# First stage of an AdaLN transformer block: q, k, v from two fp32r parts in three products, the norm on ScalarE, statistics two units ahead

## The chip, the core and the metric

The kernel runs on one core of a Trainium2 chip, with five engines that run programs of their own and meet at semaphores: TensorE (matmuls, into PSUM), VectorE (DVE), ScalarE (ACT), GpSimd (POOL) and SyncE (SP), which here only issues DMAs. The metric is the time of one execution on the device in microseconds, the median of several.

## What is computed

```python
mod = (silu(c) @ wmod).reshape(B, 6, 1, -1)          # sa, ca, ga, sb, cb, gb
h = layernorm(x) * (1 + ca) + sa                     # x: 4 x 2048 x 256
qkv = h @ w_qkv                                      # w_qkv: 256 x 768, 16 heads of 16
q, k = rope(q), rope(k)
x = x + ga * (softmax(causal(q @ k.T * scale)) @ v @ w_proj + b_proj)
h = layernorm(x) * (1 + cb) + sb
x = x + gb * (routed_experts(h) + shared_expert(h))  # 8 experts, 2 per row
```

All of it is fp32 in its inputs and outputs. The change touches the first `h` and `qkv` alone.

## The kernel before

It has stages: setup, `qkv_stage`, attention, a middle stage (projection, second norm, routing), the experts and the shared expert, with a barrier between stages. `setup_stage` loads the weights (`wqkv`, 128 x 2 x 768), the rope tables and the first rows of `x`, and computes the modulation vectors; it ends when DVE has written the rows `mod_rows`.

`qkv_stage` works on 16 units of 512 rows (`ST`), four tiles (`TPS`) of 128 rows in each; four units (`SPB`) are a batch. `steps_of` gives every engine the same order: for each unit u, iterations t = 0 to 3, and within one iteration an engine works on tile t for the early steps and on tiles t-2 and t-3 (of the unit before, where negative) for the late ones. `tile(t, k)` names the tile k iterations back. In one iteration, for the tiles t, t-2, t-3:

- TensorE: `products` (L629 to L641) writes q and k (512 columns) and v (256 columns) of tile t into PSUM, two `matmul` each over the two halves c of the 256 input columns; then `turn_qk` (L643) transposes q and k of tile t-2. At t = 2 `turn_h` (L620) transposes the normalised rows of the next unit, eight blocks.
- DVE: `rope` (three operations, L536 to L539) on tile t; `leave` (L547) takes the rest of tile t-3 that the first bf16 part leaves. At t = 0, `stat` of the next unit (L511, L516) between them; at t = 1, behind them, `normalise` (L522), four operations that write `xn`.
- GpSimd: `add` (L483, rope's sum) for tile t; at t = 0 `rstds` (L475, L477: variance to 1/sqrt); `third` (L487, the third bf16 part) for tile t-3.
- ScalarE: at t = 2 `modulate` (L574) first, two activations that take the transposed rows from PSUM, scale and shift them and write `h_t`; then `take_v` (L582) for tile t, `first` (L589) for t-2, `second` (L594) for t-3.
- SyncE loads `x` (three units ahead) and stores v and the bf16 parts of q and k of each unit.

Semaphores that matter here: `products` of tile n waits for `rope` and `take_v` of tile n-2 (two PSUM buffers). `turn_qk` of tile n waits for `add(n)` and for `leave` of tile n-2. `leave(n)` waits for `first(n)`, `second(n)` for `leave(n)`, `third(n)` for `second(n)`. `turn_h` waits for `xn_done` tile by tile, `modulate` for `ht_turned`. `products` of a unit's first tile waits for both `modulate` of that unit.

The fp32 matmuls here appear as two records each. The expert and the shared stage already split fp32 operands into two fp32r parts, high and low (`PARTS`), and add three products, high*high, low*high and high*low (`PRODUCTS`). The middle stage normalises on ScalarE (L1410), with a shift computed on DVE.

Of the kernel before, what the change touches and what calls it, by code (L numbers as in the profile page):

```python
# [24 lines left out]
F32 = mybir.dt.float32  # L25
# [65 lines left out]
def block_kernel(nc, x, w_qkv, w_proj, b_proj, gate_w, w_gate, w_up, w_down, sw_gate, sw_up, sw_down,  # L91
# [27 lines left out]
    with ExitStack() as whole:  # L119
# [17 lines left out]
        with ExitStack() as front:  # L137
# [7 lines left out]
            with ExitStack() as first:  # L145
# [3 lines left out]
                    wqkv=first.enter_context(nc.sbuf_tensor("wqkv", [P, DC, 3 * D], F32)),  # L149
# [31 lines left out]
def setup_stage(nc, C, Q, A, ident_dram, cond, wmod, gate_w, x_flat, w_qkv, cos_dram, sin_dram):  # L181


    with ExitStack() as ctx:
# [34 lines left out]
        def _(sp):  # L219
# [7 lines left out]
            sp.dma_start(Q["wqkv"][:, :, :], w_qkv.rearrange("(c p) n -> p c n", p=P)).then_inc(Q["consts"], 16)  # L227
# [11 lines left out]
        def _(pool):  # L239
# [73 lines left out]
def qkv_stage(nc, C, Q, x_flat, rows_mod_dram, qk_dram, v_dram):  # L313
# [9 lines left out]
    def steps_of(run, engine):  # L323
# [13 lines left out]
        for u in range(-1, SPB):  # L337
            run(u // SPB, u % SPB, within(u)(1), around(u // SPB, u % SPB, within(u)))
        with engine.Fori(1, B - 1) as b:
            for s in range(SPB):  # L340
                run(b, s, True, around(b, s, lambda k: True))
        for u in range((B - 1) * SPB, NST + 1):
            run(u // SPB, u % SPB, within(u)(1), around(u // SPB, u % SPB, within(u)))

    with ExitStack() as ctx:
# [16 lines left out]
        xn = sb("xn", [P, 2, TPS, D])  # L362
        h_t = sb("h_t", [P, 2, DC, ST])
# [21 lines left out]
        ht_done = sem("p1_ht")  # L385
        qk_done = sem("p1_qk")
# [76 lines left out]
        def _(pool):  # L463
# [8 lines left out]
            def rstds(u):  # L472
# [3 lines left out]
                pool.wait_ge(pool_own, u + 3)  # L476
                pool.tensor_tensor(rstd[:, :], var[:, :], power[:, :], ALU.pow).then_inc(rstd_done, 1)  # L477
# [12 lines left out]
            def run(b, s, more, tile):  # L490
# [12 lines left out]
        def _(v):  # L503
            v.sem_inc(x_read, SPB)
            v.sem_inc(rope_done, TPS)
            v.sem_inc(rest_done, 2)

# [42 lines left out]
            def run(b, s, more, tile):  # L550
                for t in range(TPS):
                    if tile(t, 0):
                        rope(b * SPB + s, t, s * TPS + t)
                    if t == 0 and more:
                        stat(b * SPB + s + 1, (s + 1) % SPB, b + ((s + 1) // SPB + 1))
# [3 lines left out]
                    if t == 1 and more:  # L559
                        normalise(b * SPB + s + 1, (s + 1) % 2, (s + 1) % SPB)  # L560
# [5 lines left out]
        def _(act):  # L566
# [3 lines left out]
            def modulate(u, slot, b):  # L570
                for c in range(DC):
                    act.wait_ge(ht_turned, u * DC + (c + 1))
                    stand_alone(act, held)
                    act.activation(h_t[:, slot, c, :], ps_ht[:, c, :], ACT.Identity,  # L574
                                   bias=mod_t[:, M_SA + c, ds(b, 1)], scale=mod_t[:, M_CA + c, ds(b, 1)]) \
                        .then_inc(ht_done, 1)
# [20 lines left out]
            def run(b, s, more, tile):  # L597
# [1660 lines left out]
```

## Time and profile before

| | us |
|---|---|
| median of 3 runs (3251.26 to 3252.61) | 3251.39 |
| profiled execution | 3249.14 |
| its span, first to last instruction | 3247.4 |

| engine | busy us of the span | share |
|---|---|---|
| TensorE, matmuls | 2902.9 | 89% |
| TensorE, weight loads | 1623.5 | 50% |
| DVE | 2519.7 | 78% |
| ScalarE | 1590.0 | 49% |
| GpSimd | 887.7 | 27% |

The mean granted clock of TensorE is 0.945 of 2.4 GHz. In the rows, times are microseconds from the start of the span unless a column says ns. In a timeline, `x4` merges four like instructions and the text in brackets is the idle time of the engine ahead of them with what ended it. "f32" in a matmul's row stands for fp32r operands too: the names with `_high` and `_low` are fp32r. Overlapping instructions count once in a busy time, so that busy us divided by the count can be below the mean length.

### The profile page before, as it was taken

The page shows a single profiled execution, that of the slowest core. Times are in us where ns is not written, and L with a number is a line of the kernel's source. Part 1 is how long each engine was busy: PE and PEld are TensorE (multiplying, and loading weights), DVE is VectorE, ACT ScalarE, POOL GpSimd, SP SyncE. Part 2 cuts the span into 40 slices and gives each one's busy share as a digit, 9 for nine tenths or more (in the row PEclk, how much of TensorE's full clock was granted, in tenths as well). Part 3 has the DMA queues.
Part 4 walks back from the last instruction along what each step waited for, and adds up shares of the span by engine and source line. Part 5 has one row for each costly group of instructions (what it writes and reads, how often), then busy time and mean ns, then how long its engine had stood idle before and what let it go on. Part 6 is the DMA issues. An engine that isn't in the chain of part 4 may idle for free. (4 is left out here: it accounts for less than half of the span.)

```text
span 3247.4 us, 61337 instructions
## 1 busy us (share of the span) xinstructions
PE 2902.9 (89%) x22508; PEld 1623.5 (50%) x22508; DVE 2519.7 (78%) x4677; ACT 1590.0 (49%) x2160; POOL 887.7 (27%) x1101
## 2 busy tenths in 40 slices
PE   6885699999999999999999997886599999989998
PEld 3553133333333333333333323675488888878887
DVE  5885998888988889888899841665477777768787
ACT  2442176666666666666666674222244444422111
POOL 5774010111101111011110111455322222245453
PEclk9997599999999999999999998776799999999999
DMA  4776211212112121121211102664654555423332
GB/s 133 207 205 189 60 29 49 55 49 58 33 48 54 49 58 34 48 52 49 58 36 47 42 8 75 188 204 148 203 157 157 157 157 157 137 93 127 101 121 81
DMA packets 388532, 317.92 MB, mean 98 GB/s; under 512 B 112720, under 2 KB 374844, under 8 KB 388288
## 3 DMA queue, kind: packets, MB, share of 16 engines
q1 hardware_dynamic: 370752, 277.67, 29.8%
q0 software_dynamic: 12288, 33.57, 3.1%
q10 hardware_dynamic: 5248, 3.41, 0.4%
q8 instruction: 155, 2.54, 0.3%
q14 instruction: 89, 0.73, 0.1%
HBM read 196.89 MB, written 116.93 MB: 97 GB/s over the span
## 5 line engine op out<-in xcount | busy, mean ns | idle before, releaser
L918 ACT ACTIVATE probs<-ps_s 128x1024 f32<-128x1024 f32 (+3 forms) x1280 | 1077.9, 896 | 598.8 <-PE ps_s L1086 598.2
L941 DVE TENSOR_REDUCE piece_rest<-ps_m 128x1 f32<-128x512 f32 (+2 forms) x1260 | 749.2, 647 | 91.4 <-PE ps_m L1061 42.4
L1086 PE MATMUL ps_s<-q_st,k_st 50*128 50x512 bf16 (+7 forms) x5120 | 594.4, 346 | 19.0 <-ACT probs L918 15.2
L898 POOL TENSOR_SCALAR_AFFINE_SELECT probs<-probs 128x256 f32<-128x256 f32 x512 | 205.0, 406 | 1480.8 <-ACT probs L918 1475.6
L1101 PE MATMUL ps_o<-probs,vs 128*32 128x512 f32 (+3 forms) x5120 | 600.5, 541 | 4.3 <-POOL probs L898 1.2
L941 DVE TENSOR_REDUCE piece_late<-ps_m 128x1 f32<-128x512 f32 x900 | 549.2, 667 | 32.4 <-PE ps_m L1053 17.1
L1053 PE MATMUL ps_m<-k_st,q_st 48*128 48x512 bf16 (+3 forms) x2400 | 407.4, 352 | 65.9 <-DVE piece_rest L941 48.1
L1053 PEld LDWEIGHTS ps_m<-k_st,q_st 48*128 48x128 bf16 x2400 | 106.8, 93 | 651.6 <-DVE piece_rest L941 339.1
L1086 PEld LDWEIGHTS ps_s<-q_st,k_st 50*128 50x128 bf16 (+1 forms) x5120 | 224.1, 95 | 250.8 <-ACT probs L918 91.1
L1829 ACT ACTIVATE act_g<-ps_g 128x512 f32<-128x512 f32 x117 | 69.9, 597 | 279.6 <-PE ps_u L1931 279.6
L2107 ACT ACTIVATE act_g<-ps_g 128x512 f32<-128x512 f32 x80 | 47.9, 598 | 277.9 <-PE ps_u L2204 249.0
L1871 DVE TENSOR_TENSOR hid_f<-act_g,ps_u 128x512 f32<-128x512 f32 x117 | 80.5, 688 | 126.9 <-ACT act_g L1829 126.9
L1101 PEld LDWEIGHTS ps_o<-probs,vs 128*32 128x32 f32 x5120 | 101.2, 108 | 142.8 <-issue 96.9
L1789 POOL TENSOR_TENSOR wu_low<-wu,wu_high 128x768 fp32r<-128x768 f32 x39 | 76.8, 1969 | 326.1 <-ACT wu_high L1817 326.1
L1372 POOL DMA_INDIRECT expert_rows<-rows,at x128 | 128.2, 1001 | 74.2 <-DVE at L1484 39.7
L2072 POOL DMA_INDIRECT got<-expert_made,at_now x128 | 132.8, 1038 | 38.5 <-issue 31.4
L1876 DVE TENSOR_TENSOR hid_low<-hid_f,hid_high 128x512 fp32r<-128x512 f32 x117 | 138.9, 1187 | 4.0
L1943 PE MATMUL ps_d<-wd_high,hid_high 128*128 128x256 f32 x468 | 136.0, 291 | 1.2 <-DVE hid_low L1876 1.2
L1943 PE MATMUL ps_d<-wd_low,hid_high 128*128 128x256 f32 x468 | 132.1, 282 | 0.0
L1943 PE MATMUL ps_d<-wd_high,hid_low 128*128 128x256 f32 x468 | 132.0, 282 | 0.0
L636 PE MATMUL ps_qk<-wqkv,h_t 128*128 128x512 f32 x256 | 122.3, 601 | 1.0 <-ACT h_t L574 1.0
L2146 DVE TENSOR_TENSOR hid_f<-act_g,ps_u 128x512 f32<-128x512 f32 x80 | 54.8, 686 | 78.5 <-ACT act_g L2107 61.6
(230 smaller groups left out, 5167.2 us busy)
## 6 DMA issues: line engine op xcount, KB each, us to landing
k_st<-qk_parts SPq DMA_DIRECT2D x768, 32.0 KB, 1.8
qk_parts<-parts SPq DMA_DIRECT2D x124, 192.0 KB, 2.9
q_st<-qk_parts SPq DMA_DIRECT2D x720, 32.0 KB, 1.8
x_r<-expert_rows SPq DMA_DIRECT2D x39, 512.0 KB, 4.5
expert_made<-made SPq DMA_DIRECT2D x39, 512.0 KB, 2.9
x_in<-in_L_attn_x_dram SPq DMA_DIRECT2D x32, 512.0 KB, 4.7
vs<-v_ones SPq DMA_DIRECT2D x64, 256.0 KB, 3.7
v_ones<-v_out SPq DMA_DIRECT2D x60, 256.0 KB, 4.7
```

The lines of the kernel that those rows point to most:

```text
L636: pe.matmul(ps_qk[:, t % 2, :], h_t[:, slot, c, t * P:(t + 1) * P], wqkv[:, c, 0:QK], start=(c == 0), stop=(c == DC - 1))
L898: pool.affine_select(out=block_now, in_=block_now, compare_op=ALU.is_ge, fill=0.0, base=0, pattern=[[0, 2], [1, P]], channel_multiplier=-1 ...
L918: act.activation(probs[:, u % PSLOTS, 2 * pair:2 * pair + 2, j * P:ST], ps_s[:, pair, :, j * P:ST], ACT.Exp, scale=SCALE).then_inc(exp_don ...
L941: v.tensor_reduce(dst, ps_m[:, bank, 0:n * w].rearrange("p (n w) -> p n w", n=n), AX.X, ALU.max) \
L1053: last[z] = pe.matmul(bank[:, i * w:(i + 1) * w], q_st[rows, slot, 0, a + i, qi * P:(qi + 1) * P], k_st[rows, slot, 0, a + i, kt * ST:kt * ...
L1086: last = pe.matmul(ps_s[:, pair, z, j * P:ST], k_st[rows, slot, half, pair, kc * P:(kc + 1) * P], q_st[rows, slot, half, pair, qt * ST + j ...
L1101: last = pe.matmul(ps_o[h * VW:(h + 1) * VW, j * P:ST], vs[:, slot, kc, h * VW:(h + 1) * VW], probs[:, u % PSLOTS, h, j * P:ST], start=(kc ...
L1372: pool.indirect_dma_start(rows_dram, bass.IndirectOffsetOnAxis(at[:, rslot, j:j + 1], 0), rows[:, rslot, j % TPS, :], None).then_inc(scatt ...
L1871: v.tensor_tensor(hid_f[:, half, :], act_g[:, half, :], ps_u[:, half, :], ALU.mult).then_inc(product, 1)
L1876: v.tensor_tensor(hid[1][:, i, :], hid_f[:, half, :], hid[0][:, i, :], ALU.subtract).then_inc(hid_done, 1)
L1943: last = pe.matmul(ps_d[:, t, :], hid[a][:, i, t * P:(t + 1) * P], wd_p[b][:, slot, i, :], start=(i == 0 and t % 2 == 0 and k == 0), stop= ...
L2072: pool.indirect_dma_start(got[:, slot, j, :], None, made_dram, bass.IndirectOffsetOnAxis(at_now[:, slot, j:j + 1], 0)) \
```

## The change

In setup the weights land in `w_raw`; ScalarE copies them to fp32r (`wqkv[0]`), GpSimd subtracts this from `w_raw` (`wqkv[1]`). In `qkv_stage` ScalarE's `modulate` writes each half twice, as fp32r (`h_p[0]`) and as fp32 (`h_f`), and DVE's new `low_rows` subtracts one from the other (`h_p[1]`). `products` does three products of two parts where it did one fp32 product. The norm goes from DVE to ScalarE as an activation with scale `rstd` and bias `shift`; DVE's new `shifts` computes `shift`. The statistics and `rstds` run two units ahead, at t = 3, on DVE ahead of `rope(3)`. `normalise` stands at the end of ScalarE's t = 0, `turn_h` at the end of TensorE's t = 1, `modulate` of half 0 at the end of ScalarE's t = 1 and of half 1 in t = 2 behind `take_v`, `shifts` at the end of DVE's t = 0 and `low_rows` at the end of its t = 2. `products` of a unit's first tile now waits for both `low_rows`. `xn` has one buffer instead of two. `steps_of` begins one unit earlier, and `has(k)` says whether unit u + k exists.

```diff
# setup_stage
-            sp.dma_start(Q["wqkv"][:, :, :], w_qkv.rearrange("(c p) n -> p c n", p=P)).then_inc(Q["consts"], 16)
+            sp.dma_start(Q["w_raw"][:, :, :], w_qkv.rearrange("(c p) n -> p c n", p=P)).then_inc(Q["consts"], 16)
...
+            pool.wait_ge(masks, 6)
+            pool.wait_ge(exp_done, 2)
+            pool.tensor_tensor(Q["wqkv"][1][:, :, :], Q["w_raw"][:, :, :], Q["wqkv"][0][:, :, :], ALU.subtract)
...
+            act.wait_ge(Q["consts"], 16 * 3)
+            act.activation(Q["wqkv"][0][:, :, :], Q["w_raw"][:, :, :], ACT.Copy).then_inc(exp_done, 1)
# qkv_stage, GpSimd
                 pool.wait_ge(pool_own, u + 3)
+                if not (isinstance(u, int) and u == 0):
+                    pool.wait_ge(xn_done, u * TPS)
+                    stand_alone(pool, held)
                 pool.tensor_tensor(rstd[:, :], var[:, :], power[:, :], ALU.pow).then_inc(rstd_done, 1)
...
-                    if t == 0 and more:
-                        rstds(b * SPB + s + 1)
+                    if t == 3 and has(2):
+                        rstds(b * SPB + s + 2)
# qkv_stage, DVE
-            def normalise(u, slot, x_slot):
+            def shifts(u):
                 v.wait_ge(rstd_done, u + 1)
-                for t in range(TPS):
-                    ins = v.tensor_scalar(xn[:, slot, t, :], x_in[:, x_slot, t, :], mv[:, t, 0:1], rstd[:, t:t + 1],
-                                          ALU.subtract, ALU.mult)
-                    ins.then_inc(xn_done, 1)
-                v.wait_ge(xn_done, (u + 1) * TPS)
-                v.sem_inc(x_read, 1)
+                v.scalar_tensor_tensor(shift[:, :], mv[:, :, 0], -1.0, rstd[:, :], ALU.mult, ALU.mult) \
+                    .then_inc(shift_done, 1)
+
+            def low_rows(u, slot, c):
+                v.wait_ge(ht_done, u * DC + (c + 1 + 2))
+                v.tensor_tensor(h_p[1][:, slot, c, :], h_f[:, c, :], h_p[0][:, slot, c, :], ALU.subtract).then_inc(h_low, 1)
...
                 for t in range(TPS):
+                    if t == 3 and has(2):
+                        stat(b * SPB + s + 2, (s + 2) % SPB, b + ((s + 2) // SPB + 1))
                     if tile(t, 0):
                         rope(b * SPB + s, t, s * TPS + t)
-                    if t == 0 and more:
-                        stat(b * SPB + s + 1, (s + 1) % SPB, b + ((s + 1) // SPB + 1))
                     if tile(t, 3):
                         u, tt, slot, _ = tile(t, 3)
                         leave(u, tt, slot)
-                    if t == 1 and more:
-                        normalise(b * SPB + s + 1, (s + 1) % 2, (s + 1) % SPB)
+                    if t == 0 and has(1):
+                        shifts(b * SPB + s + 1)
+                    if t == 2 and has(1):
+                        for c in range(DC):
+                            low_rows(b * SPB + s + 1, (s + 1) % 2, c)
# qkv_stage, ScalarE
+            def modulate(u, slot, b, c):
+                act.wait_ge(ht_turned, u * DC + (c + 1))
+                act.wait_ge(h_low, u * DC + (c + 1))
+                stand_alone(act, held)
+                act.activation(h_p[0][:, slot, c, :], ps_ht[:, c, :], ACT.Identity,
+                               bias=mod_t[:, M_SA + c, ds(b, 1)], scale=mod_t[:, M_CA + c, ds(b, 1)])
+                act.activation(h_f[:, c, :], ps_ht[:, c, :], ACT.Identity,
+                               bias=mod_t[:, M_SA + c, ds(b, 1)], scale=mod_t[:, M_CA + c, ds(b, 1)]) \
+                    .then_inc(ht_done, 1)
+
+            def normalise(u, slot, x_slot):
+                act.wait_ge(shift_done, u + 1)
+                stand_alone(act, held)
+                for t in range(TPS):
+                    act.activation(xn[:, t, :], x_in[:, x_slot, t, :], ACT.Identity,
+                                   bias=shift[:, t:t + 1], scale=rstd[:, t:t + 1]).then_inc(xn_done, 1)
+                act.wait_ge(xn_done, (u + 1) * TPS)
+                act.sem_inc(x_read, 1)
...
                 for t in range(TPS):
-                    if t == 2 and more:
-                        modulate(b * SPB + s + 1, (s + 1) % 2, b + (s + 1) // SPB)
                     if tile(t, 0):
                         take_v(b * SPB + s, t, s % 2, b * 2 + (s // 2 + 1))
+                    if t == 2 and has(1):
+                        modulate(b * SPB + s + 1, (s + 1) % 2, b + (s + 1) // SPB, 1)
...
+                    if t == 0 and has(1):
+                        normalise(b * SPB + s + 1, (s + 1) % 2, (s + 1) % SPB)
+                    if t == 1 and has(1):
+                        modulate(b * SPB + s + 1, (s + 1) % 2, b + (s + 1) // SPB, 0)
# qkv_stage, TensorE
                 if t == 0:
-                    pe.wait_ge(ht_done, u * DC + (DC + 2))
+                    pe.wait_ge(h_low, u * DC + 2 * DC)
...
+                terms = [(c, a, b) for c in range(DC) for a, b in PRODUCTS]
+                for k, (c, a, b) in enumerate(terms):
+                    pe.matmul(ps_qk[:, t % 2, :], h_p[a][:, slot, c, t * P:(t + 1) * P], wqkv[b][:, c, 0:QK],
+                              start=(k == 0), stop=(k == len(terms) - 1))
+                for k, (c, a, b) in enumerate(terms):
+                    last = pe.matmul(ps_v[:, t % 2, 0:D], h_p[a][:, slot, c, t * P:(t + 1) * P], wqkv[b][:, c, QK:3 * D],
+                                     start=(k == 0), stop=(k == len(terms) - 1))
...
-                    if t == 2 and more:
+                    if t == 1 and has(1):
                         turn_h(b * SPB + s + 1, (s + 1) % 2)
```

## Rows read from the trace of the kernel before

**Rows 1.** one unit: busy us of PE, PEld, DVE, ACT, POOL; clock; DMA

```profile
165.10:180.35 15.25, 13.60 (x58) 8.45 (x57) 12.54 (x29) 7.33 (x14) 10.93 (x11) 1.00 0.77 207
```

**Rows 2.** timeline of one unit, TensorE: start, length, engine, line, operation, count, idle before

```profile
182.74 0.63 PE L648 MATMUL ps_x<-ident,qk 128*128 128x128 f32 x4 [0.94 <-DVE rest L547]
...
188.26 1.88 PE L636 MATMUL ps_qk<-wqkv,h_t 128*128 128x512 f32 x4
...
191.28 1.88 PE L636 MATMUL ps_qk<-wqkv,h_t 128*128 128x512 f32 x4
...
193.87 0.60 PE L648 MATMUL ps_x<-ident,qk 128*128 128x128 f32 x4
...
194.30 1.88 PE L636 MATMUL ps_qk<-wqkv,h_t 128*128 128x512 f32 x4
```

**Rows 3.** timeline, TensorE, at the start and at the end of the stage

```profile
37.86 3.78 PE L636 MATMUL ps_qk<-wqkv,h_t 128*128 128x512 f32 x4 [0.96 <-ACT h_t L574]
...
51.02 1.88 PE L636 MATMUL ps_qk<-wqkv,h_t 128*128 128x512 f32 x4
...
276.59 1.88 PE L636 MATMUL ps_qk<-wqkv,h_t 128*128 128x512 f32 x4
```

**Rows 4.** timeline of the same unit, DVE

```profile
180.09 1.39 DVE L511 BATCH_NORM_STATS2 stats<-x_in 128x6 f32<-128x256 f32 x4
...
181.94 0.66 DVE L547 TENSOR_TENSOR rest<-ps_x,parts 128x512 f32<-128x512 f32 x1
...
184.37 3.24 DVE L522 TENSOR_SCALAR xn<-x_in,mv,rstd 128x256 f32<-128x256 f32 x4
...
191.05 0.69 DVE L536 TENSOR_TENSOR rot_c<-ps_qk,cos 128x512 f32<-128x512 f32 x1 [1.18 <-PE ps_v L639]
...
192.32 0.68 DVE L547 TENSOR_TENSOR rest<-ps_x,parts 128x512 f32<-128x512 f32 x1
```

**Rows 5.** timeline of the expert stage, TensorE: fp32r products, 512 columns, then 256

```profile
2320.03 0.40 PE L1931 MATMUL ps_g<-x_t_low,wg_high 128*128 128x512 f32 x1
...
2322.11 0.39 PE L1931 MATMUL ps_u<-x_t_low,wu_high 128*128 128x512 f32 x1
...
2323.08 0.28 PE L1943 MATMUL ps_d<-wd_high,hid_high 128*128 128x256 f32 x1
...
2324.04 0.28 PE L1943 MATMUL ps_d<-wd_high,hid_low 128*128 128x256 f32 x1
```

**Rows 6.** groups of instructions by line: shapes, count, busy us, mean ns, idle before

```profile
L1410 ACT ACTIVATE xn<-x,shift,rstd 128x256 f32<-128x256 f32 x64 | 33.0, 592 | 1.2 <-DVE shift L1448 1.2
...
L574 ACT ACTIVATE h_t<-ps_ht,mod_t 128x512 f32<-128x512 f32 x32 | 23.2, 773 | 74.6 <-PE ps_ht L626 74.5
...
L2152 DVE TENSOR_TENSOR hid_low<-hid_f,hid_high 128x512 fp32r<-128x512 f32 x80 | 55.5, 693 | 2.8
```

**Rows 7.** timeline of the same unit, GpSimd and ScalarE

```profile
182.22 0.23 POOL L475 TENSOR_SCALAR var<-mv 128x4 f32<-128x4 f32 x1 [0.62 <-DVE mv L516]
...
183.54 1.16 POOL L487 TENSOR_TENSOR parts<-rest,parts 128x512 bf16<-128x512 f32 x1
...
192.56 1.27 POOL L483 TENSOR_TENSOR qk<-rot_c,rot_s 128x512 f32<-128x512 f32 x1 [0.47 <-DVE rot_s L539]
...
193.03 0.63 ACT L594 ACTIVATE parts<-rest 128x512 bf16<-128x512 f32 x1 [0.95 <-DVE rest L547]
```

**Rows 8.** timeline of the expert stage, GpSimd and DVE

```profile
2329.51 1.97 POOL L1793 TENSOR_TENSOR wd_low<-wd,wd_high 128x768 fp32r<-128x768 f32 x1 [1.54 <-ACT wd_high L1820]
...
2329.82 2.21 DVE L1876 TENSOR_TENSOR hid_low<-hid_f,hid_high 128x512 fp32r<-128x512 f32 x1
```

**Rows 9.** GpSimd: the stage's first instruction, in the timeline; a subtraction, by line

```profile
28.37 3.52 POOL L464 MEMSET v_out<- 128x4096 f32 x1 [12.55 <-POOLq L184]
...
L1801 POOL TENSOR_TENSOR sd_low<-sd_w,sd_high 128x1536 fp32r<-128x1536 f32 x1 | 3.4, 3419 | 14.8 <-ACT sd_high L1846 14.8
```

**Rows 10.** busy time of each engine in a stretch of the middle stage

```profile
2050.00:2055.00 5.00, 3.77 (x13) 2.90 (x12) 3.84 (x32) 3.16 (x7) 3.02 (x4) 0.50 1.06 250
```

More of the change, by code:

```diff
@@ L148, in block_kernel @@
                     sin=first.enter_context(nc.sbuf_tensor("sin", [P, NT, HD], F32)),
-                    wqkv=first.enter_context(nc.sbuf_tensor("wqkv", [P, DC, 3 * D], F32)),
+                    wqkv=[first.enter_context(nc.sbuf_tensor(f"wqkv_{part}", [P, DC, 3 * D], F32R)) for part in PARTS],
+                    w_raw=first.enter_context(nc.sbuf_tensor("wqkv_raw", [P, DC, 3 * D], F32)),
                     x_in=first.enter_context(nc.sbuf_tensor("x_in", [P, SPB, TPS, D], F32)),
@@ L335, in within @@
             return lambda k: 0 <= u + k < NST
-        for u in range(-1, SPB):
-            run(u // SPB, u % SPB, within(u)(1), around(u // SPB, u % SPB, within(u)))
+        for u in range(-2, SPB):
+            run(u // SPB, u % SPB, within(u), around(u // SPB, u % SPB, within(u)))
         with engine.Fori(1, B - 1) as b:
             for s in range(SPB):
-                run(b, s, True, around(b, s, lambda k: True))
+                run(b, s, lambda k: True, around(b, s, lambda k: True))
         for u in range((B - 1) * SPB, NST + 1):
-            run(u // SPB, u % SPB, within(u)(1), around(u // SPB, u % SPB, within(u)))
+            run(u // SPB, u % SPB, within(u), around(u // SPB, u % SPB, within(u)))
     with ExitStack() as ctx:
@@ L361, in qkv_stage @@
         power = sb("power", [P, TPS])
-        xn = sb("xn", [P, 2, TPS, D])
-        h_t = sb("h_t", [P, 2, DC, ST])
+        xn = sb("xn", [P, TPS, D])
+        h_p = [sb(f"h_{part}", [P, 2, DC, ST], F32R) for part in PARTS]
+        h_f = sb("h_f", [P, DC, ST])
+        shift = sb("shift1", [P, TPS])
         rot_c = sb("rot_c", [P, TPS, QK])
@@ L488, in third, with run @@
                                    parts[:, slot, 1, :, t * P:(t + 1) * P], ALU.subtract).then_inc(part3, 1)
-            def run(b, s, more, tile):
+            def run(b, s, has, tile):
                 for t in range(TPS):
@@ L506, in _ @@
             v.sem_inc(rest_done, 2)
+            v.sem_inc(h_low, DC)
             def stat(u, slot, turn):
@@ L548, in leave, with run @@
                                 parts[:, slot, 0, :, t * P:(t + 1) * P], ALU.subtract).then_inc(rest_done, 1)
-            def run(b, s, more, tile):
+            def run(b, s, has, tile):
                 for t in range(TPS):
+                    if t == 3 and has(2):
+                        stat(b * SPB + s + 2, (s + 2) % SPB, b + ((s + 2) // SPB + 1))
                     if tile(t, 0):
                         rope(b * SPB + s, t, s * TPS + t)
-                    if t == 0 and more:
-                        stat(b * SPB + s + 1, (s + 1) % SPB, b + ((s + 1) // SPB + 1))
                     if tile(t, 3):
@@ L595, in second, with run @@
                     .then_inc(part2, 1)
-            def run(b, s, more, tile):
+            def run(b, s, has, tile):
                 for t in range(TPS):
-                    if t == 2 and more:
-                        modulate(b * SPB + s + 1, (s + 1) % 2, b + (s + 1) // SPB)
                     if tile(t, 0):
                         take_v(b * SPB + s, t, s % 2, b * 2 + (s // 2 + 1))
+                    if t == 2 and has(1):
+                        modulate(b * SPB + s + 1, (s + 1) % 2, b + (s + 1) // SPB, 1)
                     if tile(t, 2):
@@ L631, in products @@
                 if t == 0:
-                    pe.wait_ge(ht_done, u * DC + (DC + 2))
+                    pe.wait_ge(h_low, u * DC + 2 * DC)
                 pe.wait_ge(rope_done, n + TPS - 1)
                 pe.wait_ge(v_done, n + 1)
-                for c in range(DC):
-                    pe.matmul(ps_qk[:, t % 2, :], h_t[:, slot, c, t * P:(t + 1) * P], wqkv[:, c, 0:QK],
-                              start=(c == 0), stop=(c == DC - 1))
-                for c in range(DC):
-                    last = pe.matmul(ps_v[:, t % 2, 0:D], h_t[:, slot, c, t * P:(t + 1) * P], wqkv[:, c, QK:3 * D],
-                                     start=(c == 0), stop=(c == DC - 1))
+                terms = [(c, a, b) for c in range(DC) for a, b in PRODUCTS]
[5 more added lines that the diff above has]
+                                     start=(k == 0), stop=(k == len(terms) - 1))
                 last.then_inc(qk_done, 1)
@@ L649, in turn_qk, with run @@
                 last.then_inc(turned, 1)
-            def run(b, s, more, tile):
+            def run(b, s, has, tile):
                 for t in range(TPS):
```

11 lines of the change are left out of this document (3 added, 8 removed).

## The prediction

> **What bounds the kernel now.** I read the page's slices first: the first stage is the first tenth of the span, everything behind it is untouched, so the question is how much earlier or later the first stage ends. Next the windows of one unit of 512 rows [rows 1]: TensorE 13.60 us busy of 15.25, DVE 12.54, GpSimd 10.93, ScalarE 7.33, DMA 0.77, granted clock 1.00. The period is (188.26 - 51.02) / 9 units = 15.25 us [rows 2, 3]. Then the timeline of that unit, engine by engine. In tiles without extra work `products` follows `products` at 3.02 us (191.28, 194.30), of which 2.59 is `products` and 0.43 `turn_qk` [rows 2]; TensorE never waits there, and DVE waits for it (1.18 us before `rot_c`) [rows 4]. Four such tiles are 12.1 us. The rest is the norm: `turn_qk` waited 0.94 us for a `leave` that stood behind the statistics, and `turn_h` had to wait for `xn`, whose last part ends at 187.61, 0.65 ahead of the next `products` [rows 2, 4]. So TensorE bounds the stage, with DVE close: its four tiles take 1.95 us each (191.05 to the end of `rest`, 193.00), the statistics 1.85 (180.09 to 181.94) and `xn` 3.24 [rows 4], 12.9 in all.
>
> **What the change takes from TensorE.** fp32 `products` is 2.59 us. The fp32r products of the expert stage start 0.23 us apart at 512 columns (nine from 2320.03 to 2322.11) and 0.12 at 256 (eight from 2323.08 to 2324.04), each with its own weights [rows 5]. A tile now has six of each: 6 x 0.23 + 6 x 0.12 = 2.10 us. With `turn_qk` a tile is 2.53, a unit 4 x 2.53 + about 1.2 for `turn_h` = 11.3 us. If TensorE stayed the bound, this would be worth 14 units x 3.9 = 55 us. It doesn't stay the bound.
>
> **What it adds and moves, per unit.** DVE loses `xn` (3.24) and gains `shifts` (a few elements, about 0.2, no row of stage one; below 1.2 with a wait) and two `low_rows`, 0.69 each where nothing is in the way [rows 6]. ScalarE gains four norm activations at 33.0/64 = 0.516 us, 2.07, and two more modulations at 23.2/32 = 0.725, 1.45 [rows 6]: 7.3 + 3.5 = 10.8 of 15 us. GpSimd keeps its 10.9. The DMA work stays 0.77 x 15.25 = 11.7 us a unit. No engine's own sum reaches 15.25, so only the chain between them decides.
>
> **The chain, walked.** Put 0 where DVE ends the second `low_rows` of a unit; u' is the next unit, in which tile 0' runs. `products(0')` starts at 0.1.
> - DVE has in its queue: statistics to 1.85, rope of tile 3 to 3.20 (1.95 less the 0.6 of `leave`), `leave(0)` to 3.80, rope and `leave(1)` of the next iteration to 5.75 [rows 4]. TensorE waits for `leave(0)` ahead of `turn_qk(2)`, from 2.2 to 3.95.
> - GpSimd: `add(3)` starts 0.16 behind the rope, at 3.36, takes 1.27; `rstds` takes 1.32 (182.22 to 183.54), to 5.95. At that moment its `third(0)` starts, as at 183.54 right after the rstd, and runs 1.16, to 7.1 [rows 7].
> - `shifts` needs rstd, so not before 5.95. It reads two SBUF operands. DVE operations of this kind wait for GpSimd: `hid_low` started at 2329.82 beside a GpSimd subtraction from 2329.51 to 2331.48, and ended at 2332.03, 2.21 us instead of 0.69 [rows 6, 8]. So `shifts` ends at 7.1, not at 6.1.
> - ScalarE has done `second(1)` at 5.78 + 0.63 = 6.41 [rows 7], the norm starts at 7.15 behind `shifts`, ends at 9.22. `products` starts 0.65 behind the last `xn` (187.61, 188.26) [rows 2, 4]: `products(2')` at 9.87.
> - It ends with 2.10 + 0.23 (the rope starts 2.79 behind `products` now, 188.26 and 191.05, and 2.59 less a small gap of that is issue) at 12.20. Rope and `leave(3)` end at 14.15. `add(2')` runs from 13.71 to 14.98 and holds up the first `low_rows`: it ends 0.55 behind GpSimd, 15.5, the second at 16.2. Their inputs are there: ScalarE goes from 9.3 through `take_v`, `first`, `second` (some 1.7 with gaps), the pair for half 0 (1.45), `take_v` (0.4) and the pair for half 1 (1.45) to about 14.5.
> - `products(0'')` waits for that. The period is 16.2 us, against 15.25.
>
> What stood on TensorE is faster, but it now waits twice in each unit for a round through DVE, GpSimd and ScalarE, and the two `low_rows` stand between one unit's norm and the next unit's products. Without either wait for GpSimd the same walk gives 14.85; with only the one at `low_rows`, 15.5; with a third, `third(3)` slipping between the two `low_rows`, 17.3. I take 16.2: both waits are with GpSimd operations that the order of the semaphores puts at just that place.
>
> **Start and end.** The split of the weights lies in the setup. GpSimd was idle for 12.55 us before the stage and a subtraction of 128x1536 takes it 3.42 [rows 9]; ScalarE's copy, by 0.63 for 512 columns [rows 7], an estimated 1.9. Cost nothing, at most 2 us if the weights land late. The first products come later: the norm on ScalarE +0.6, two modulations more +1.45, `low_rows` +0.69, so 37.86 + 2.7 = 40.6. At the lower clock (3.78 us for four matmuls that take 1.88 later [rows 2, 3]) the first tile takes about 3.9, then 0.23, rope 1.35, shift 0.2, norm 2.07, 0.65: `products(2)` of unit 0 at 49.0, against 51.02 [rows 3]. Then 14 periods. From there 6.3 to the last `low_rows`, and the last unit has no statistics and no norm: 0.1 + 3 x 2.53 to the last `products`, 14.0 in all; it is 0.46 shorter. Before, the last `products` starts at 276.59 [rows 3]. Difference at the stage's end: 49.0 + 14P + 14.0 - 0.5 - 276.6 = 14P - 214.1. With P = 16.2: +12.7 us. What follows (the last stores, the barrier, attention) moves as a block; I cost it at 0, within 3 us.
>
> The profiled execution took 3249.14 us (span 3247.4), the median is 3251.39, so 2.25 more: 3251.4 + 12.7 = 3264.
>
> **The rivals.**
> - Only one wait for GpSimd counts (a shift of four elements slips in): P = 15.5, +2.9 us, 3254. For it: no row shows so small an operation held up. Chance 0.22.
> - The round is shorter, ending on the other side. Its place is the norm: if it starts at 6.4 and `low_rows` is not held up, P = 14.85, -6 us, 3245; it is faster from P below 15.3 on. In the extreme the queues drift so that the round never closes, and TensorE at 11.3 or DMA at 11.7 us bounds: -50 us, 3200. Against it: DVE really has 5.75 us of queued work behind `low_rows`. Chance 0.16, nearly all of it at the near end, a quarter inside 0.2%.
> - TensorE's clock. In stage one it was 1.00 with TensorE at 13.60 of 15.25 [rows 1]. In the middle stage a stretch with TensorE at 3.77 of 5 us had 0.50, the level of 1.2 GHz [rows 10]. After the change TensorE has some 11.3 of 16.2 and, ahead of `products(2')`, over 3 us with only 12 transposes. If the clock falls there, `products(2')` takes 4.2, P = 18.3, +42 us, 3293. Chance 0.18. The Trainium skill, "TensorE: Matmul & The Clock Gate", section "Part 1: The HAM clock gate", says that the throttled level is the default and activity releases it; by that rule this rival is what happens once the stalls are long enough, 3293. By [rows 1] alone it doesn't happen, 3264.
> - The change doesn't do what it says: fp32r products no faster in this layout (weights and rows swapped in their roles against the expert stage). Then a tile costs three times 2.56, a unit 4 x 8.1 + 1.2 = 33.6, +257 us, about 3508. Chance 0.02.
> - The forecast: P = 16.2 with its neighbours 15.8 to 16.8, 3258 to 3272. Chance 0.42.
>
> On the waits for GpSimd the Trainium skill, "SBUF — State Buffer", section "SBUF: two separate sides", says that the port pair the two share is an exclusive lock for the whole instruction, also for a VectorE operation with two SBUF inputs against a GpSimd one that reads SBUF. The 2.21 us of [rows 8] agree. It speaks against this change, since `low_rows` and `shifts` are of this kind and replace, in `xn`, an operation that took 3.24 for four beside GpSimd [rows 4]: by it the forecast stands, without it the sum would be 14.85 a unit.
>
> **Numbers.** 3264. Range 3242 to 3295: below it lies half of the shorter round, above it the upper part of the clock's case. 0.2% is 6.5 us, about what a measurement of this kernel can tell from no change. Faster 0.12, same 0.27 (one wait only, part of the shorter round), slower 0.61 (forecast, clock, no gain from fp32r).
>
> **What would show it.** Right: products 2.1 us; `turn_qk(2)` waiting near 1.8 us for `leave`, `turn_h` over 1 us for `xn` now from ScalarE; `products` of tile 0 waiting for `low_rows`; `low_rows` above 0.69 on the mean, one of each pair; `shifts` up to 1.2; period 16.2; clock 1.00. Wrong: a clock under 1.00 between 60 and 280 us; a period under 15; `low_rows` and `shifts` at their bare time; TensorE without waits, or DMA near 1.0. It is most easily wrong in the phase between GpSimd and DVE, since each wait there is up to 1.2 us, times 14.

## The result, and the profile after

The changed kernel takes 3276.39 us (six runs, 3269.27 to 3286.84) beside 3250.06 us of the kernel before on the same chip (six runs, 3246.42 to 3252.61): a ratio of 1.0084, 95% interval [1.0063, 1.0104]. It is 26.3 us slower. The forecast was 3264, so 12.7 us slower, with a range of 3242 to 3295: the direction is right, the time lies inside the range, and the loss is twice the forecast's.

The page of the changed kernel, its totals and the granted TensorE clock in slices of 82 us:

```profile
span 3279.5 us, 61996 instructions
...
PE 2900.8 (88%) x22764; PEld 1667.1 (51%) x22764; DVE 2530.3 (77%) x4661; ACT 1642.2 (50%) x2257; POOL 895.1 (27%) x1102
...
PEclk8889599999999999999999998776699999999999
```

Three dots stand for lines left out. The first four slices of the last line hold the first stage; its clock is 0.8 to 0.9. The place of the loss is found by the instruction with which attention begins on GpSimd. Timeline of GpSimd, changed kernel:

```profile
328.25 0.22 POOL L923 MEMSET piece_rest<- 128x144 f32 x1 [11.94 <-POOLq L351]
```

Before, this memset started at 299.16. The first stage is 29.1 us longer. What follows takes 3279.5 - 328.25 = 2951.3 us, before it was 3247.4 - 299.16 = 2948.2. So the first stage holds the loss, and nothing beyond 3 us is lost behind it, as forecast. That it came out so close is partly luck: the work behind the stage is the same in every kernel of this document, and in the other profiles it took from 2945.8 to 2964.8 us, with 2947.5 and 2961.3 for two kernels on one chip (e5_no_lock, e8_fp32_products). A difference of a few us is therefore read from the stage, not from the total. (The two profiled executions, 3281.26 and 3249.14, are 32.1 us apart, somewhat more than the medians.)

Busy time in three units of the changed kernel and in one shorter stretch (columns as in [rows 1]):

```profile
177.25:194.50 17.25, 13.75 (x72) 11.35 (x72) 13.38 (x28) 10.52 (x20) 11.23 (x10) 0.90 0.68 182
229.00:247.65 18.65, 15.34 (x72) 12.68 (x72) 13.37 (x28) 10.52 (x20) 11.23 (x10) 0.82 0.64 169
247.65:264.80 17.15, 12.33 (x72) 10.07 (x72) 13.20 (x28) 10.40 (x20) 11.16 (x10) 1.00 0.70 185
...
195.20:198.40 3.20, 3.19 (x11) 2.54 (x10) 2.91 (x11) 0.10 (x1) 0.57 (x1) 0.50 0.86 215
```

A unit took 15.25 us and now takes 17.02 to 17.26, with two of 18.59 and 18.65. The mean over 13 units is 17.39. No engine is full: at clock 1.00 TensorE has 12.33 of 17.15 us, DVE 13.20 (in which its waits for GpSimd count as busy), the DMA engines fell from 0.77 to 0.70 [rows 1]. That is the picture of a round of waits, in which each engine waits for the next, and not of one engine that sets the pace.

The round is in the timeline of the unit from 177.25. Answering to [rows 2, 4, 7], DVE first, then GpSimd, ScalarE, TensorE:

```profile
177.25 1.39 DVE L525 BATCH_NORM_STATS2 stats<-x_in 128x6 f32<-128x256 f32 x4
...
180.33 0.68 DVE L561 TENSOR_TENSOR rest<-ps_x,parts 128x512 f32<-128x512 f32 x1
...
183.38 1.12 DVE L535 SCALAR_TENSOR_TENSOR shift<-mv,rstd 128x4 f32<-128x4 f32 x1
...
189.66 0.69 DVE L550 TENSOR_TENSOR rot_c<-ps_qk,cos 128x512 f32<-128x512 f32 x1 [3.30 <-PE ps_v L672]
...
191.53 3.04 DVE L540 TENSOR_TENSOR h_low<-h_f,h_high 128x512 fp32r<-128x512 f32 x2
```

```profile
182.31 1.04 POOL L490 TENSOR_TENSOR rstd<-var,power 128x4 f32<-128x4 f32 x1 [0.26 <-POOL var L485]
183.32 1.17 POOL L500 TENSOR_TENSOR parts<-rest,parts 128x512 bf16<-128x512 f32 x1
...
191.18 1.30 POOL L496 TENSOR_TENSOR qk<-rot_c,rot_s 128x512 f32<-128x512 f32 x1 [1.66 <-DVE rot_s L553]
192.50 1.53 POOL L500 TENSOR_TENSOR parts<-rest,parts 128x512 bf16<-128x512 f32 x1
```

```profile
184.62 2.08 ACT L601 ACTIVATE xn<-x_in,shift,rstd 128x256 f32<-128x256 f32 x4 [0.68 <-DVE shift L535]
```

```profile
181.09 0.84 PE L681 MATMUL ps_x<-ident,qk 128*128 128x128 f32 x4
...
187.27 0.48 PE L669 MATMUL ps_qk<-wqkv_high,h_high 128*128 128x512 f32 x1
...
189.82 0.48 PE L669 MATMUL ps_qk<-wqkv_high,h_high 128*128 128x512 f32 x1
...
194.63 0.50 PE L669 MATMUL ps_qk<-wqkv_high,h_high 128*128 128x512 f32 x1 [2.02 <-DVE h_low L540]
```

Read it as one chain. The second `low_rows` ends (177.3); DVE does statistics, rope, `leave(0)`, rope, `leave(1)`; GpSimd has rstd at 183.35 and goes on with `third(0)` to 184.49; `shift` sits through it and ends at 184.50; the norm on ScalarE ends at 186.70; `products(2')` starts at 187.27 and the next tile's at 189.82, 2.55 later; DVE, idle for 3.30 us, does the rope; the two `low_rows` take from 191.53 to 194.57 while GpSimd runs `add` and then `third`; the `products` of the next unit's first tile wait 2.02 us for them. Then the same again.

### The profile page after: what moved, and what is told of

The parts are those of the page before. It is cut to its first block and busy times, and to the rows that moved or that the text cites. A ratio compares the mean times of both kernels' runs of the same rounds, so it can differ in the third digit from the quotient of the medians.

```text
span 3279.5 us, 61996 instructions
## 1 busy us (share of the span) xinstructions
PE 2900.8 (88%) x22764; PEld 1667.1 (51%) x22764; DVE 2530.3 (77%) x4661; ACT 1642.2 (50%) x2257; POOL 895.1 (27%) x1102
## 5 line engine op out<-in xcount | busy, mean ns | idle before, releaser
L1119 PE MATMUL ps_s<-q_st,k_st 50*128 50x512 bf16 (+7 forms) x5120 | 594.4, 346 | 19.0 <-ACT probs L951 15.2
L1094 PE MATMUL ps_m<-mask,ident 64*128 64x128 bf16 x1920 | 113.1, 215 | 0.0
```

The lines of the kernel that those rows point to most:

```text
L1119: last = pe.matmul(ps_s[:, pair, z, j * P:ST], k_st[rows, slot, half, pair, kc * P:(kc + 1) * P], q_st[rows, slot, half, pair, qt * ST + j ...
```

## The experiments

Each is the changed kernel with the edit named; where code is shown it is an excerpt. "Period" is the mean length of the units of 512 rows in the steady part (11 to 13 of them), "stage" the time at which attention's memset starts, both from one profile of each kernel. The ratio is to the kernel before on the same chip, whose median differs a little between the chips (3250 to 3261 us), so ratios and stages are compared. The changed kernel has 1.0084, 17.39 and 328.25, the kernel before 15.25 and 299.16.

**The low part read from PSUM.** ScalarE writes the fp32 value in place in PSUM, so that `low_rows` has only one SBUF source. The transposes of the next unit now wait for `low_rows` to be done with the bank.

```
-   act.activation(h_f[:, c, :], ps_ht[:, c, :], ACT.Identity,
+   act.activation(ps_ht[:, c, :], ps_ht[:, c, :], ACT.Identity,
...
-   v.tensor_tensor(h_p[1][:, slot, c, :], h_f[:, c, :], h_p[0][:, slot, c, :], ALU.subtract)
+   v.tensor_tensor(h_p[1][:, slot, c, :], ps_ht[:, c, :], h_p[0][:, slot, c, :], ALU.subtract)
```

> The changed kernel, but ScalarE writes the fp32 copy of h back into PSUM, in place of the transposed rows, and low_rows reads it there: one SBUF operand instead of two, the same results. Theory A (the waits of DVE for GpSimd's SBUF operations sit on the unit's round): each low_rows takes 0.69 us instead of 1.54 on the mean, the period falls from 17.3 to about 15.5 us, 14 times 1.8 is 25 us, so about 3251, level with the kernel before. Rival B (the fallen TensorE clock of the first stage is what costs the 26 us): low_rows gets shorter, but the clock still falls, and the time stays above 3268.

Measured 1.0054 [1.0032, 1.0075], period 16.21, stage 311.68. The group of `low_rows` by line, then two units, all of this kernel:

```profile
L539 DVE TENSOR_TENSOR h_low<-ps_ht,h_high 128x512 fp32r<-128x512 f32 x26 | 16.6, 680 | 0.0
```

```profile
71.23:88.13 16.90, 13.90 (x72) 11.31 (x72) 11.52 (x28) 10.37 (x21) 10.84 (x11) 0.90 0.70 188
104.97:120.31 15.34, 12.38 (x72) 10.06 (x72) 11.52 (x28) 10.41 (x21) 10.82 (x11) 1.00 0.76 207
```

`low_rows` falls from 1543 ns on the mean (28 of them, changed kernel) to 680: the wait for GpSimd is gone. Six units take 15.33 to 15.48, as the walk with only the other wait says (15.5). Seven take 16.8 to 17.0 and show a clock of 0.90. In the one shown, TensorE goes through the norm's transposes with short waits, the longest 0.90 us, and `products(2')` behind them runs at 0.50, the level of 1.2 GHz. Two windows of 1 us of this kernel, at that `products`:

```profile
81.20:82.20 1.00, 1.00 (x5) 0.57 0.63 193
82.20:83.20 1.00, 1.00 (x3) 0.50 1.03 339
```

So the price of the wait was right, and the rival of the clock is real too: in all seven long units, and in none of the six others, the `products` behind the transposes ran at the lower level. The total came out between the two theories, 1.0054 where level was expected; its eight runs spread over 22 us (3263.28 to 3285.34).

**Both halves in one `low_rows`.** This takes away the gap into which `third` slips. The one operation now waits for both halves at once.

```
+   v.wait_ge(ht_done, u * DC + (DC + 2))
+   v.tensor_tensor(h_p[1][:, slot, :, :], h_f[:, :, :], h_p[0][:, slot, :, :], ALU.subtract).then_inc(h_low, DC)
```

> The changed kernel with one low_rows of 1024 columns instead of two of 512. Theory A: the GpSimd subtraction third can't slip in between the two any more; what is left is the wait for add and 1.22 us of work. Period 17.3 - 1.1 = 16.2, 14 x 1.1 = 15 us less, about 3261. If the second wait is not on the round: no change, 3276.

Measured 1.0089 [1.0072, 1.0106], period 17.10, stage 325.22. Group and two units of this kernel:

```profile
L540 DVE TENSOR_TENSOR h_low<-h_f,h_high 128x1024 fp32r<-128x1024 f32 x13 | 25.8, 1987 | 0.0
```

```profile
125.30:141.51 16.21, 12.35 (x72) 10.07 (x72) 12.24 (x27) 10.41 (x20) 11.79 (x11) 1.00 0.74 196
141.51:159.33 17.82, 13.94 (x72) 11.35 (x72) 12.26 (x28) 10.41 (x20) 11.79 (x11) 0.90 0.67 177
```

The pair goes from 3.04 to 1.99 us, and the five units at clock 1.00 take 15.99 to 16.23: the forecast's 16.2. The other eight take 17.6 to 17.8 at 0.90, again the units whose `products` behind the transposes ran at the lower level. So the clock takes back most of what the gap gave. The stage ends 3.0 us earlier and the ratio doesn't move; the total of about 3261 that was expected, 15 us less, was missed.

**The shift on GpSimd**, behind rstd, so that DVE has nothing to wait for there.

```
+   pool.tensor_scalar(minus[:, :], mv[:, :, 0], -1.0, None, ALU.mult)
    (rstd)
+   pool.tensor_tensor(shift[:, :], minus[:, :], rstd[:, :], ALU.mult).then_inc(shift_done, 1)
```

> The changed kernel with the shift of the norm computed on GpSimd, behind the reciprocal root, instead of on DVE, where it takes 1.12 us instead of 0.16. Theory A: the norm starts some 0.6 to 0.9 us earlier, period 16.5, 9 to 13 us less, about 3265. Rival: the norm is not on the round (only low_rows is), then 3276 as it was.

Measured 1.0076 [1.0059, 1.0093], period 16.74, stage 320.42. The groups by line of this kernel, and of the changed one:

```profile
L495 POOL TENSOR_TENSOR shift<-minus,rstd 128x4 f32<-128x4 f32 x14 | 2.8, 199 | 2.5 <-POOL rstd L492 2.5
```

```profile
L535 DVE SCALAR_TENSOR_TENSOR shift<-mv,rstd 128x4 f32<-128x4 f32 x14 | 15.7, 1120 | 4.9 <-POOL rstd L490 4.6
```

Four elements in 1120 ns on DVE, 199 on GpSimd. All units lie between 16.6 and 16.9, the period falls by 0.65: the wait at the shift lies on the round, as the forecast has it. Of the 0.65, some 0.2 come from the two units of over 18.5 us, which this kernel doesn't have; like against like it is 17.25 to 16.82, 0.43 us, and not 1.1. The timelines say why. In one unit of this kernel:

```profile
151.97 3.04 DVE L542 TENSOR_TENSOR h_low<-h_f,h_high 128x512 fp32r<-128x512 f32 x2
```

```profile
160.35 1.04 POOL L492 TENSOR_TENSOR rstd<-var,power 128x4 f32<-128x4 f32 x1
161.57 0.20 POOL L495 TENSOR_TENSOR shift<-minus,rstd 128x4 f32<-128x4 f32 x1 [0.18 <-POOL rstd L492]
```

```profile
161.89 2.08 ACT L601 ACTIVATE xn<-x_in,shift,rstd 128x256 f32<-128x256 f32 x4 [0.63 <-POOL shift L495]
```

The norm starts 6.9 us behind the end of `low_rows` (155.01), where it was 7.3 (177.33 to 184.62). The new instruction for `minus` sets rstd back by 0.4 (5.3 us behind `low_rows` instead of 5.0), and the shift follows it with 0.18 and 0.20 us. The edit takes away the hold of 1.1 us and pays most of it on GpSimd. The ratio, 1.0076, shows less than the 9 to 13 us that were expected; the stage is 7.8 us shorter.

**Both waits away** (the first and the third edit together).

> Both waits of DVE for GpSimd taken out: fp32 h in PSUM (as in e1) and shift on GpSimd (as in e3). By the walk of the prediction a unit at the full clock takes 14.85 us, against 15.33 to 15.48 in the undisturbed units of e1 and 16.8 in e3; units in which the clock falls after turn_h take 1.4 us more. If no clock fell: a bit below the kernel before, ratio 0.998; with half the units struck, 1.001. If the walk is wrong and something else closes the round, the undisturbed units stay at 15.4.

Measured 0.9989 [0.9975, 1.0002], period 15.00, stage 293.77. One unit of it:

```profile
128.38:143.43 15.05, 12.36 (x72) 10.08 (x72) 10.48 (x28) 10.37 (x21) 11.22 (x13) 1.00 0.78 212
```

All units are between 14.90 and 15.11 with clock 1.00; the walk without either wait said 14.85. With the two waits gone, and with them the falls of the clock, the slowdown is gone: the rest is no change, or a little less than before. Why the clock falls no more isn't shown by this run (see "Open" below).

**The clock by itself.** The kernel that reads from PSUM, with seven extra matmuls around the transposes, so that TensorE rests less there. They are matmuls of 512 columns, wait only for the rope of tile 0, and write the bank of PSUM that this rope has read and that `products` starts anew.

```
    for _ in range(4 if t == 0 else 1):
        pe.matmul(ps_qk[:, 0, :], wqkv[0][:, 0, 0:P], wqkv[0][:, 0, 0:QK], start=True, stop=True)
```

> e1 with seven extra matmuls of 512 columns around the wait for xn in turn_h (four ahead of it, one behind each of three transposes); they write a PSUM buffer that products overwrites, the results are the same. Theory A (the units of 16.8 to 17.0 us in e1 are those in which TensorE's clock falls after turn_h): clock 1.00 throughout, all units at 15.3 to 15.6, ratio 1.001 against 1.0054 of e1. Rival D (these units are long for another reason, DMA traffic for one, and the clock falls because of it): the long units stay.

Measured 1.0003 [0.9986, 1.0021], period 15.42, stage 300.86. One unit:

```profile
131.61:147.10 15.49, 13.77 (x79) 11.04 (x79) 11.51 (x29) 10.38 (x21) 10.90 (x11) 1.00 0.77 205
```

All units are 15.32 to 15.49 at clock 1.00, against 15.4 or 16.9 without the matmuls. More work on TensorE made the kernel faster, and the other reading of the long units, that something else lengthens them and the clock follows, is ruled out.

**The same for the changed kernel itself**: seven matmuls around the transposes and seven ahead of the wait for `low_rows`.

> The changed kernel itself with the extra matmuls of e6, and seven more ahead of the wait for low_rows. In its profile the clock fell in 11 of 13 units but only two of these were 1.4 us longer, since where it falls in the others TensorE waits for leave anyway. So: clock 1.00, period 17.0 to 17.3, ratio 1.007 to 1.008. If the clock cost more than that in the runs without a profile: ratio below 1.005.

Measured 1.0083 [1.0067, 1.0100], period 17.18, stage 325.85:

```profile
140.49:157.76 17.27, 15.41 (x86) 12.26 (x86) 13.29 (x29) 10.41 (x20) 11.28 (x10) 1.00 0.69 183
```

The clock is 1.00 in every unit, and the ratio is that of the changed kernel (1.0084). In the changed kernel the clock falls mostly behind the wait for `low_rows`. The stretch 195.20 to 198.40 above has it at 0.50, but `turn_qk` behind that `products` has to wait for `leave(0)`, until 198.26, anyway. Only the two units of 18.6 pay for it, 1.4 us each, which is 3 of 3276 us.

**Statistics behind `leave`**, so that TensorE doesn't wait for `leave(0)` behind them.

> The changed kernel with the statistics at the end of DVE's iteration 3, behind rope and leave, instead of ahead of them. TensorE's wait for leave ahead of turn_qk (0 to 1.6 us) goes. Theory A (the round runs through DVE's queue, where rope, leave and statistics have the same sum up to the norm): little moves, within 10 us of 3276, and what moves comes from the shift, which meets GpSimd at another moment. Rival C (TensorE's visible wait at that place is what costs): 14 x 1.5 = 20 us less, about 3255.

Measured 1.0088 [1.0066, 1.0109], period 17.10, stage 325.19. TensorE's waits for `leave` fall from 7.2 us in all to 3.0, and the ratio doesn't move. The mean hides two kinds of units of this kernel:

```profile
107.70:124.33 16.63, 13.93 (x75) 11.67 (x74) 13.27 (x29) 10.62 (x20) 11.22 (x11) 0.90 0.71 191
124.33:142.56 18.23, 13.94 (x72) 11.30 (x71) 13.19 (x28) 10.56 (x20) 11.28 (x11) 0.88 0.65 174
```

Nine take 16.5 to 17.0, less than the changed kernel's 17.02 to 17.26. The one from 142.56, DVE and then ScalarE:

```profile
137.74 3.04 DVE L540 TENSOR_TENSOR h_low<-h_f,h_high 128x512 fp32r<-128x512 f32 x2
```

```profile
147.50 2.08 ACT L601 ACTIVATE xn<-x_in,shift,rstd 128x256 f32<-128x256 f32 x4 [0.52 <-DVE shift L535]
```

The norm starts 6.7 us behind the end of `low_rows` (140.78 to 147.50) instead of 7.3, because the statistics, now behind `leave`, leave GpSimd free to do `add(3)` first, and its rstd is there after 5.4 us instead of 6.0. The four others take 17.8 to 18.2, and they are those in which the `products` behind the transposes ran at the lower level.

**The new order with the old products.** fp32 products from one fp32 `h`, no `low_rows`; statistics, shift and norm where the change puts them.

> The new order (norm on ScalarE, statistics two units ahead) with the old fp32 products: modulate writes one fp32 h, no low_rows, products waits for modulate. Theory A (low_rows between one unit's norm and the next unit's products closes the round, the order alone does not): TensorE bounds again, 4 x 3.02 + 1.2 + 0.9 of waiting for xn, period 14.2, ratio 0.995. Rival E (moving the norm to ScalarE is what costs): period above 15.25, ratio above 1.000.

Measured 0.9983 [0.9963, 1.0002], period 14.70, stage 291.71:

```profile
155.79:170.54 14.75, 13.82 (x57) 8.58 (x56) 10.43 (x26) 9.35 (x18) 10.75 (x11) 1.00 0.85 224
```

The order alone costs nothing (if anything it gains a little, though less than the period of 14.2 that was expected); here TensorE is again close to full. The cheaper products with what they need, two `low_rows` and two more modulations, bring the 2.7 us a unit.

**Where the slack can be used.** Two attempts to break the round, built on the kernel without the two waits. The first does statistics, rstd and norm one tile or more earlier, so that the transposes find `xn` ready; the transposes go to tile 0 and `low_rows` stands ahead of `leave`.

> e5 in another order: statistics at the end of DVE's iteration 1, where it waited for products, reciprocal root and shift on GpSimd in iteration 2, norm on ScalarE at the end of iteration 3 of the unit before, turn_h at the end of iteration 0, low_rows ahead of leave. Theory A (the round through DVE's queue to the norm sets the period, no engine's sum does): with the norm off the round, the period falls to between 12.3 and 13.5 us, near the sums (TensorE 11.3, DVE 11.5, GpSimd 11.6, DMA 11.7), some 14 x 2.3 = 32 us below the kernel before, ratio 0.990. Rival: DMA or the split itself bounds, period above 15.

Measured 1.0122 [1.0085, 1.0159], period 18.49, stage 338.27: a miss. Timeline of SyncE's queue and of DVE in it:

```profile
191.27 0.41 SPq L432 DMA_DIRECT2D x_in<-in_L_attn_x_dram  x1
```

```profile
196.01 1.41 DVE L531 BATCH_NORM_STATS2 stats<-x_in 128x6 f32<-128x256 f32 x4 [2.02 <-DMA x_in<-in_L_attn_x_dram]
```

The load of x is issued by SyncE behind the stores of the unit before, and the statistics, now earlier, wait for it 12 times, 27.5 us in all, 3.2 at most. The second attempt adds to this one that the load is issued a unit earlier, ahead of a wait for the last part of q and k.

> e7 with only the loads of x moved ahead of the stores of q and k. Theory: of e7's 18 us a unit the 2.0 to 3.2 us in which DVE waited for x go, and the clock falls less often; 14.5 to 16 us a unit, ratio about 1.001. If the statistics ahead of rope(2) and low_rows ahead of leave are harmless, it comes down to 12 to 13 instead.

Measured 1.0078 [1.0061, 1.0095], period 17.15, stage 324.03: missed again. The wait for x is gone, but the engines still wait for each other. Timelines of GpSimd, ScalarE and TensorE:

```profile
174.81 0.23 POOL L486 TENSOR_SCALAR var<-mv 128x4 f32<-128x4 f32 x1
...
177.04 2.08 ACT L603 ACTIVATE xn<-x_in,shift,rstd 128x256 f32<-128x256 f32 x4 [1.70 <-POOL shift L495]
```

```profile
177.70 0.33 PE L661 MATMUL ps_ht<-ident,xn 128*128 128x128 f32 x1 [1.09 <-ACT xn L603]
```

The order wanted the norm a tile ahead; it runs just in front of its transposes. As I read the timeline, that is because the statistics come behind rope, `low_rows` and `leave` on DVE, and rstd behind `third` on GpSimd; how much of the 17.15 is which of these is not separated.

The last one has the earlier load and spreads the links: statistics at the end of tile 0, rstd and shift in tile 1, the norm in tile 3 of the unit before, transposes at tile 0, the modulations at the ends of tiles 0 and 1, one `low_rows` at the ends of tiles 1 and 2 each.

```
-   if t == 2 and has(1): (both low_rows)
+   if t in (1, 2) and has(1):
+       low_rows(b * SPB + s + 1, (s + 1) % 2, t - 1)
```

> e7 with its two new waits taken out: SyncE loads x ahead of the stores of q and k instead of behind them, and DVE's extra work is spread: statistics at the end of iteration 0, one low_rows at the end of iteration 1 and one at the end of 2, behind leave; modulate at the end of 0 and 1. Theory A: no round goes through the norm or low_rows, the period comes down to the sums, 12.0 to 12.9 us (DMA 11.7, GpSimd 11.6, TensorE 11.4), 14 x 2.7 = 38 us less than before, ratio 0.989. Rival F (the early norm itself costs, whatever the loads): period above 15.

Measured 3226.27 us, 0.9896 [0.9874, 0.9918], stage 262.02. Eleven units of it in one window:

```profile
70.35:211.24 140.89, 133.57 (x800) 111.52 (x800) 117.51 (x287) 114.67 (x224) 124.35 (x135) 1.00 0.94 248
```

140.89 / 11 is 12.81 us a unit, with the DMA engines at 0.94 and TensorE at 133.57 of 140.89. The same fp32r products that made the stage 29.1 us longer make it 37.1 us shorter than before (299.16 to 262.02). This version beats both kernels. Between it and the one without the two waits (293.77) only places in the order differ. Which of the moves gave the most wasn't run, nor was this order with fp32 products; with them TensorE alone was busy for 13.82 us a unit (e8_fp32_products), so an estimated 1.0 us a unit of this result, at least, needs the cheaper products.

## Why the prediction was right, and where it was off

The direction and the cause were right, the size was half of what came. 3276 lies outside the forecast's own neighbourhood (3258 to 3272, P up to 16.8), and its being inside the range owes something to luck: the room above was kept for the clock, which cost 3 us, while a third wait for GpSimd filled it.

**fp32r products: right.** 2.10 us and 2.53 with `turn_qk` were forecast, and the tiles start 2.55 apart (187.27, 189.82).

**TensorE doesn't stay the bound: right.** Of the 3.9 us a unit that the cheaper products free, nothing arrives: the order alone with fp32 products takes 14.70 a unit, the changed kernel 17.39.

**The walk, from the end of a unit's second `low_rows`: right in each step but the last.** Forecast beside the unit from 177.3:

| step | forecast | measured |
|---|---|---|
| `leave(0)` ends | 3.80 | 3.7 |
| `leave(1)` ends | 5.75 | 6.0 |
| rstd | 5.95 | 6.05 |
| shift ends | 7.1 | 7.2 |
| norm ends | 9.22 | 9.4 |
| `products(2')` | 9.87 | 9.97 |
| rope of it starts | 12.20 | 12.36 |
| `leave(3)` ends | 14.15 | 14.3 |
| `add(2')` | 13.71 to 14.98 | 13.9 to 15.2 |
| second `low_rows` ends | 16.2 | 17.27 |

**The mis-sized term is the last one**: "it ends 0.55 behind GpSimd, 15.5, the second at 16.2". I let the first `low_rows` wait for `add` and gave the second its bare 0.69. In the trace `third(3)` starts at 192.50, 0.02 behind the end of `add`, while the pair of `low_rows` isn't through. It takes 1.53 us instead of 1.17, and the pair ends 0.54 behind it, after 3.04 us instead of some 2.0. The line shown merges the pair; that `third` runs between the two is read from these lengths. The forecast's sign, "one of each pair" above 0.69, has it wrong in the same way: both were held, 1543 ns on the mean, and the longest took 1769 ns of a pair's 3.04 us. The case stands in the prediction as a variant, "a third, `third(3)` slipping between the two `low_rows`, 17.3", and was not taken. Kernel e2_low_in_one takes only this gap away, and its undisturbed units take 16.2. The error is 1.05 us x 14 = 15 us, which is the distance from 12.7 to 26.3 within 2 us; the two units that the clock struck are 3 more.

**Shift: right.** 1.12 us on the mean, through `third(0)`. Without it the period is 0.65 lower, and not 1.0, since the way round it costs GpSimd time ahead of the norm (see the experiment).

**The sum.** "14P - 214.1" with P = 17.39 gives +29.4, the stage measured +29.1. It holds for other kernels too: e1_low_from_psum +12.8 against +12.5, e5_no_lock -4.1 against -5.4, e8_fp32_products -8.3 against -7.5; it is furthest off for e7_norm_early, +44.8 against +39.1. The first `products` start at 41.70 (forecast 40.6), 1.0 of it because the stage's first memset starts at 29.39 instead of 28.37. The split of the weights isn't shown to be the reason: with the same setup e9_spread has this memset at 28.25 and e11_after_kept_busy at 29.84, so the start moves by itself. The split is hidden as said, to within a few tenths of a us that this spread doesn't exclude. GpSimd's subtraction took 3.43 us, the forecast's 3.42.

**The clock: the rival was half true.** A clock under 1.00 was named as a sign of being wrong, and it came: it fell in 11 of 13 units, mostly behind the wait for `low_rows` and not ahead of `products(2')`, where it had been put. Behind that wait it costs nothing, since the next step waits for DVE. Two units were struck where the rival said (18.6; it said 18.3, by a price of 2.1 us where 1.4 was measured). In one of them, TensorE, the last transposes and a matmul of `products(2')`, of 0.63 us where 0.39 is usual:

```profile
238.51 0.76 PE L658 MATMUL ps_ht<-ident,xn 128*128 128x128 f32 x5 [0.16 <-ACT xn L601]
...
239.58 0.63 PE L669 MATMUL ps_qk<-wqkv_high,h_low 128*128 128x512 f32 x1
```

[rows 1] alone, "it doesn't happen", was wrong; 3293 too, since it takes all units to be struck. With the first wait away (e1_low_from_psum) the clock costs 1.5 us in half of the units: a wait that is removed lays bare the next one. The place decides in each kernel looked at: the long units of the changed kernel (2), of e1_low_from_psum (7), of e2_low_in_one (8) and of e4_stat_behind_leave (4) are exactly those in which `products` behind the transposes ran at the lower level.

By the Trainium skill, "TensorE: Matmul & The Clock Gate", section "Part 1: The HAM clock gate", the throttled level is the default and activity releases it. With this the traces agree, and the seven extra matmuls that hold the clock at 1.00 (15.42 instead of 16.21 a unit) show it from the other side.

**One wait or two.** The rival with 3254 held that so small a shift slips in. It doesn't: 1120 ns, where the shortest of the 16 took 152. The Trainium skill, "SBUF — State Buffer", section "SBUF: two separate sides", says that the pair of ports is held for the whole instruction, whichever engine is first. The runs agree for an operation of four elements too, and with `low_rows` read from PSUM (680 ns) the wait is gone.

**Open.** Why the clock falls in seven units of e1_low_from_psum and in none of e5_no_lock, whose TensorE has as little work, is not settled; the phases of the waits differ, and no run separates them. Nor is what moves the stage's start by 1 us.

## What to carry to other kernels

Making the busiest engine faster gives time only as far as no round of waits through the other engines' queues is longer: here TensorE had 12.33 us of work in a unit of 17.15. Walk one round from rows of the old trace, with each engine's queue in order: that gave every step within 0.25 us, and the one step that missed was a pair of operations that I took as a block, while the other engine had one more operation ready for the gap. When a mean doesn't move, list the units one by one: in e2_low_in_one and e4_stat_behind_leave the shorter units and the struck ones nearly cancel in the mean. Where the sums of all engines are far below the period, move the links of the chain apart (another tile, an earlier load) before making any link cheaper: here that took a stage from 293.8 us, without the two waits, to 262.0, while two half-way versions of it ended at 324.0 and 338.3.

## What the runs showed of the hardware that was not expected

- Between two DVE operations queued back to back, with two SBUF sources each, a ready GpSimd operation gets in, as the lengths say: the pair takes 3.04 us, as one operation of the double size 1.99, with a PSUM source 0.68 each.
- The hold also strikes operations of a few elements: 128x4 in 1.12 us. In the setup, `mod_t<-mod_t` of 128x8, which reads one SBUF tile only, took 1.00 us beside GpSimd's subtraction and ended 0.02 behind it; before it took 0.17:

```profile
17.36 3.43 POOL L253 TENSOR_TENSOR wqkv_low<-wqkv_raw,wqkv_high 128x1536 fp32r<-128x1536 f32 x1 [1.53 <-ACT wqkv_high L260]
```

```profile
19.81 1.00 DVE L280 TENSOR_SCALAR mod_t<-mod_t 128x8 f32<-128x8 f32 x1
```

- TensorE's clock fell to the level of 1.2 GHz around waits of 1 to 2 us mixed with transposes, though no wait in the units was longer than 2.2 us and TensorE was busy for over 12 of 17 us. Seven more matmuls in those waits kept it at 2.4 GHz.
